# Gating the second FFN weight per batch instead of the FFN output, in an adaLN block on one Trainium2 core

## What is computed

```python
sa, ca, ga, sb, cb, gb = chunks of silu(c) @ wmod      # one row of 1024 for each batch
ga, gb = sign * max(|.|, 0.25)
h = layernorm(x) * (1 + ca) + sa
x = x + ga * gelu(h @ attn.T + b2_attn)                # attn = (w1 @ w2.T) * band mask
h = layernorm(x) * (1 + cb) + sb
P = h @ U1;  H = P @ V1 + b1                           # rank 256, 2 x 2752 columns
Z = (silu(gate) * up) @ U2                             # rank 256
x = x + gb * (Z @ V2 + b2f)                            # V2: 256 x 1024
```

## Time and profile before

| | us |
|---|---|
| median of 3 runs | 1271.64 |
| lowest, highest | 1271.54, 1274.2 |
| span of the profiled execution | 1272.8 |
| TensorE busy in it | 1200.2 |
| VectorE, ScalarE, GpSimd busy | 683.4, 388.0, 239.6 |

### The profile page before, as it was taken

How to read it: one execution, slowest core, us unless ns; L and a number is a source line. 1 busy time by engine, 2 the same in 40 slices (tenths; PEclk the granted TensorE clock), 3 DMA queues, 4 the chain that set the end, 5 groups by cost and what they waited for, 6 DMA issues and landing times.

```text
span 1272.8 us, 15879 instructions
## 1 busy us (share of the span) xinstructions
PE 1200.2 (94%) x5617; PEld 956.4 (75%) x5617; DVE 683.4 (54%) x1104; ACT 388.0 (30%) x645; POOL 239.6 (19%) x194
## 2 busy tenths in 40 slices
PE   7877999999999899999999989999999999999995
PEld 4445678877777688788878868878877887887884
DVE  0838699999996433453363353363353336336335
ACT  0122334444433454223322312223322331332230
POOL 0023322233222364120030030030011003003003
PEclk9899899999999899999999989999998999999998
DMA  9796644544447453050050031013004004003001
GB/s 347 280 382 242 238 166 182 214 181 181 192 181 272 169 169 124 28 176 1 1 182 1 1 119 64 1 57 126 1 24 160 1 1 162 20 1 115 35 1 66
DMA packets 51168, 154.71 MB, mean 122 GB/s; under 512 B 4640, under 2 KB 8992, under 8 KB 49056
## 3 DMA queue, kind: packets, MB, share of 16 engines
q1 hardware_dynamic: 51104, 153.79, 33.2%
HBM read 111.80 MB, written 41.98 MB: 121 GB/s over the span
## 4 chain that ended last, share of the span: by engine, by line
issue 56%; PE 24%; DVE 8%; POOL 8%; DMA 2%; ACT 1%; SPq 1%; POOLq 0%; DVEq 0%; ACTq 0%
POOL x2t L1360 6%; PE bank L469 5%; PE bank L471 5%; PE bank L470 5%; PE bank L539 4%; DVE nrm L1024 2%; PE bank L635 2%; DMA x<-in_x 2%; PE bank L504 1%; DVE bn L1182 1%; DVE h_lo L1125 1%; DVE bn L1014 1%; DMA wm_sb<-in_wmod 1%; POOL g L1308 1%; DVE xr L1177 1%
## 5 line engine op out<-in xcount | busy, mean ns | idle before, releaser
L1236 DVE SCALAR_TENSOR_TENSOR act<-bank,b_sb,act 128x512 f32<-128x512 f32 (+1 forms) x176 | 131.9, 750 | 411.9 <-PE bank L471 394.0
L961 ACT ACTIVATE act<-bank,b_sb 128x512 f32<-128x512 f32 (+1 forms) x176 | 121.3, 690 | 546.9 <-PE bank L471 529.3
L469 PE MATMUL bank<-pt,v_hi 128*128 128x512 f32 x688 | 270.9, 394 | 7.7 <-issue 6.2
L470 PE MATMUL bank<-pt,v_hi 128*128 128x512 f32 x688 | 269.7, 392 | 0.0
L471 PE MATMUL bank<-pt,v_lo 128*128 128x512 f32 x688 | 269.6, 392 | 0.0
L1360 POOL TENSOR_TENSOR x2t<-ffn,x2t 128x512 f32<-128x512 f32 x64 | 89.9, 1410 | 677.0 <-DVE ffn L1272 677.0
L469 PEld LDWEIGHTS bank<-pt,v_hi 128*128 128x128 f32 x688 | 130.2, 189 | 38.4 <-issue 9.6
L471 PEld LDWEIGHTS bank<-pt,v_lo 128*128 128x128 f32 x688 | 130.3, 189 | 27.3
L470 PEld LDWEIGHTS bank<-pt,v_hi 128*128 128x128 f32 x688 | 130.3, 189 | 26.8
L469 PE MATMUL bank<-act_hi,u_hi 128*128 128x512 f32 (+1 forms) x352 | 138.3, 393 | 0.9 <-DVE act_lo L1243 0.9
L471 PE MATMUL bank<-act_hi,u_lo 128*128 128x512 f32 (+1 forms) x352 | 137.0, 389 | 0.0
(11 more groups left out here) (111 smaller groups left out, 1519.5 us busy)
## 6 DMA issues: line engine op xcount, KB each, us to landing
wm_sb<-in_wmod SPq DMA_DIRECT2D x10, 2048.0 KB, 12.4
xr<-in_x SPq DMA_DIRECT2D x16, 1024.0 KB, 6.9
x_dram<-xr SPq DMA_DIRECT2D x16, 1024.0 KB, 4.4
x2t<-x_dram SPq DMA_DIRECT2D x32, 512.0 KB, 3.9
out<-x2t SPq DMA_DIRECT2D x32, 512.0 KB, 4.6
xs<-in_x SPq DMA_DIRECT2D x7, 2048.0 KB, 8.1
pt_dram<-pt_st SPq DMA_DIRECT2D x8, 1024.0 KB, 3.9
pt<-pt_dram SPq DMA_DIRECT2D x8, 1024.0 KB, 5.8
```

The costliest lines, as they stand in the source:

```text
L469: nc.tensor.matmul(acc, s_hi, m_hi, start=start, stop=False)
L470: nc.tensor.matmul(acc, s_hi, m_lo, start=False, stop=False)
L961: nc.scalar.activation(act[0:w, i % 2, :], bank[0:w, i % 2, :], ACT.Silu, bias=b1_sb[0:w, i, 0:1]).then_inc(silu_done, 1)
L1236: nc.vector.scalar_tensor_tensor(act[0:w, i % 2, :], up, b1_sb[0:w, i, 1:2], act[0:w, i % 2, :], ALU.add, ALU.mult).then_inc(act_done, 1)
```

## The change

- The gate row is multiplied into V2 for each batch. SP loads V2 into a buffer `v2g` for each batch; GpSimd multiplies it by the gate row in 4 parts of 128x512, ScalarE makes 4 high parts (`v2_hi_part`, after steps 16 to 19 of the batch), GpSimd 4 low parts. The two V2 pieces leave the weight queue. `out_product` waits for the 4 low parts of its batch.
- The row gb * b2f is computed once (`gbb2`), written to DRAM by eight small stores like the gate row, and read back broadcast for each batch. b2f comes to the core by eight small loads for this. GpSimd adds the row to the tile of x2 in place, 8 additions of 128x512 for a batch (`bias_x2`), after the low parts of V2.
- VectorE does one operation for a block: PSUM plus tile of x2, into the tile. The buffers `ffn` go, and so does the addition on GpSimd behind it.
- SP's order: loads for the next batch's V2 and rows are issued when this batch's low parts of V2 and its biased tile are done, ahead of this batch's output stores.

```diff
@@ names, sync engine @@
+            b2f_rows = c_pad[0:FB * NB].rearrange("p k c -> p (k c)")[:, 0:P]
+            gbb2_rows = b2f_rows
-        ffn = buf(p2, "ffn", [P, 3, HALF])
+        v2g = buf(p2, "v2g", [P, RB, D])
-        b2f_bc = buf(p2, "b2f_bc", [P, D])
+        gbb2_bc = buf(p2, "gbb2_bc", [P, D])
-        for h in range(NH):
-            pieces.append([(v2_view[:, :, h * HALF:(h + 1) * HALF], P, RB, HALF, 0,
-                            v2_hi[:, :, h * HALF:(h + 1) * HALF], v2_lo[:, :, h * HALF:(h + 1) * HALF])])
+        V2_PARTS = [(r, slice(h * HALF, (h + 1) * HALF)) for r in range(RB) for h in range(NH)]
+        V2_FROM = 16
             iteration(NB - 1, True, True, False, (), True)
+            sp.wait_ge(mod_mm, NCHUNK)
+            for k in range(FB):
+                sp.dma_start(b2f_rows[k * NB:(k + 1) * NB, :],
+                             b2f[:, k * P:(k + 1) * P].broadcast_to([NB, P])).then_inc(b2f_in, 16)
             for m in range(3, 7):
                 raw_load(m)
...
                 sp.dma_start(gb_dram[:, 0, k * P:(k + 1) * P], gb_rows[k * NB:(k + 1) * NB, :]).then_inc(gb_out, 16)
+            sp.wait_ge(gbb2_ready, 1)
+            for k in range(FB):
+                sp.dma_start(gbb2_dram[:, 0, k * P:(k + 1) * P],
+                             gbb2_rows[k * NB:(k + 1) * NB, :]).then_inc(gb_out, 16)
             for m in range(7, PIECES):
                 raw_load(m)
             sp.wait_ge(pt_out, 16 * NB)
-            sp.wait_ge(gb_out, 16 * FB)
-            sp.dma_start(b2f_bc[:], b2f[:, :].broadcast_to([P, D])).then_inc(b2f_in, 16)
+            sp.wait_ge(gb_out, 2 * 16 * FB)
+            def gates_in(b):
+                if not at_start(b):
+                    sp.wait_ge(v2_lo_ready, b * 4)
+                sp.dma_start(v2g[:], v2_view).then_inc(v2_in, 16)
+                sp.dma_start(gb_bc[:], gb_dram[b].broadcast_to([P, D])).then_inc(gb_in, 16)
+                if not at_start(b):
+                    sp.wait_ge(x2_biased, b * 8)
+                sp.dma_start(gbb2_bc[:], gbb2_dram[b].broadcast_to([P, D])).then_inc(gbb2_in, 16)
+            gates_in(0)
...
-                if not at_start(b):
-                    sp.wait_ge(ffn_ready, b * 8)
-                sp.dma_start(gb_bc[:], gb_dram[b].broadcast_to([P, D])).then_inc(gb_in, 16)
+                if not last:
+                    gates_in(b + 1)
@@ TensorE, out_product @@
-                pe.wait_ge(w_ready, PIECES)
+                pe.wait_ge(v2_lo_ready, b * 4 + 4)
-                        pe.wait_ge(ffn_sum, b * 8 + max(m - 1, 0))
+                        pe.wait_ge(out_ready, b * 8 + max(m - 1, 0))
@@ ScalarE @@
+            def v2_hi_part(b, part):
+                r, cols = V2_PARTS[part]
+                ae.wait_ge(v2_gated, b * 4 + part + 1)
+                if part == 0 and not at_start(b):
+                    ae.wait_ge(o_mm, b * 8)
+                nc.scalar.activation(v2_hi[:, r, cols], v2g[:, r, cols], ACT.Copy).then_inc(v2_hi_ready, 1)
                     act_hi_part(b, q, i - 1)
+                    if V2_FROM <= i < V2_FROM + 4:
+                        v2_hi_part(b, i - V2_FROM)
@@ VectorE @@
+            dve.wait_ge(gb_ready, 1)
+            dve.wait_ge(b2f_in, 16 * FB)
+            nc.vector.tensor_tensor(gbb2_rows, gb_rows[:], b2f_rows, ALU.mult).then_inc(gbb2_ready, 1)
...
-                        nc.vector.tensor_tensor(ffn[:, m % 3, :], bank[:, 6 + m % 2, :], b2f_bc[...], ALU.add)
-                        nc.vector.tensor_tensor(ffn[:, slot, :], ffn[:, slot, :], gb_bc[...], ALU.mult)
+                    half = x2t[:, n, h * HALF:(h + 1) * HALF]
+                    dve.wait_ge(o_mm, b * 8 + m + 1)
+                    dve.wait_ge(x2_biased, b * 8 + m + 1)
+                    nc.vector.tensor_tensor(half, bank[:, 6 + m % 2, :], half, ALU.add).then_inc(out_ready, 1)
@@ GpSimd @@
-                    nc.gpsimd.tensor_tensor(half, ffn[:, m % 3, :], half, ALU.add).then_inc(out_ready, 1)
+            def gate_v2(b):
+                pool.wait_ge(v2_in, b * 16 + 16)
+                pool.wait_ge(gb_in, b * 16 + 16)
+                for part, (r, cols) in enumerate(V2_PARTS):
+                    nc.gpsimd.tensor_tensor(v2g[:, r, cols], v2g[:, r, cols], gb_bc[:, cols],
+                                            ALU.mult).then_inc(v2_gated, 1)
+                for part, (r, cols) in enumerate(V2_PARTS):
+                    pool.wait_ge(v2_hi_ready, b * 4 + part + 1)
+                    nc.gpsimd.tensor_tensor(v2_lo[:, r, cols], v2g[:, r, cols], v2_hi[:, r, cols],
+                                            ALU.subtract).then_inc(v2_lo_ready, 1)
+            def bias_x2(b):
+                pool.wait_ge(gbb2_in, b * 16 + 16)
+                for m in range(TT * NH):
...
+                    nc.gpsimd.tensor_tensor(half, gbb2_bc[:, h * HALF:(h + 1) * HALF], half,
+                                            ALU.add).then_inc(x2_biased, 1)
+            with pool.Fori(0, NB) as b:
+                gate_v2(b)
+                bias_x2(b)
```

More of the change, by code:

```diff
@@ L75, in adaln_block @@
     gb_dram = nc.dram_tensor("gb_dram", [NB, 1, D], F32, kind="Internal").ap()
+    gbb2_dram = nc.dram_tensor("gbb2_dram", [NB, 1, D], F32, kind="Internal").ap()
     with ExitStack() as ctx:
@@ L251, in adaln_block @@
         o_mm = sem("o_mm")
-        ffn_sum = sem("ffn_sum")
-        ffn_ready = sem("ffn_ready")
+        v2_in = sem("v2_in")
+        v2_gated = sem("v2_gated")
+        v2_hi_ready = sem("v2_hi_ready")
+        v2_lo_ready = sem("v2_lo_ready")
+        x2_biased = sem("x2_biased")
         out_ready = sem("out_ready")
         b2f_in = sem("b2f_in")
+        gbb2_ready = sem("gbb2_ready")
+        gbb2_in = sem("gbb2_in")
         gb_in = sem("gb_in")
@@ L934, in weight_hi @@
                     ae.wait_ge(p_done, NB)
-                if m == PIECES - NH:
-                    ae.wait_ge(pt_out, 16 * NB)
                 ae.wait_ge(raw_in[m % 3], raw_count[m])
@@ L1256, in batch @@
                     multiply(b + 1, 1 - q, 0)
[L1257 to L1273, removed]
+                for m in range(TT * NH):
+                    n, h = m // NH, m % NH
+                    half = x2t[:, n, h * HALF:(h + 1) * HALF]
+                    dve.wait_ge(o_mm, b * 8 + m + 1)
+                    dve.wait_ge(x2_biased, b * 8 + m + 1)
+                    nc.vector.tensor_tensor(half, bank[:, 6 + m % 2, :], half, ALU.add).then_inc(out_ready, 1)
                     if m == 3 and not last:
@@ L1351, in _ @@
                 weight_lo(m)
-            def residual(b):
+            def gate_v2(b):
[10 more added lines that the diff above has]
+                pool.wait_ge(gbb2_in, b * 16 + 16)
                 for m in range(TT * NH):
@@ L1358, in residual @@
                         pool.wait_ge(x2t_in[n], b * 16 + 16)
-                    pool.wait_ge(ffn_ready, b * 8 + m + 1)
-                    nc.gpsimd.tensor_tensor(half, ffn[:, m % 3, :], half, ALU.add).then_inc(out_ready, 1)
+                    nc.gpsimd.tensor_tensor(half, gbb2_bc[:, h * HALF:(h + 1) * HALF], half,
+                                            ALU.add).then_inc(x2_biased, 1)
             with pool.Fori(0, NB) as b:
-                residual(b)
+                gate_v2(b)
+                bias_x2(b)
 _NAMES = ["x", "w1", "w2t", "b2", "mask", "u1", "v1", "u2", "v2", "b1_main", "b1_tail", "b2f", "ct", "wmod"]
```

## The result

| | before | after |
|---|---|---|
| median of 4 runs, us | 1272.92 | 1254.85 |
| lowest, highest | 1271.54, 1274.69 | 1254.12, 1255.44 |
| span of the profiled execution | 1272.8 | 1252.3 |
| TensorE, VectorE, ScalarE, GpSimd busy | 1200.2, 683.4, 388.0, 239.6 | 1193.5, 672.5, 402.4, 320.1 |

The ratio is 0.986, with a 95% interval of 0.9847 to 0.9874. The change makes the kernel 18.1 us faster.

The account below looks back on a forecast made before the run. TensorE, busy for 94% of the span, was taken to bound the kernel. The terms -9.3 - 6.8 + 5.6 + 1.2 = -9.3 us took the median of 1271.64 to 1262.3 us; range 1256 to 1268.5.

Parts of the forecast that it names:

- output stage, batches 0 to 6: Output products: with one VectorE addition for each block, the 1.33 us lost per batch all goes, -9.3 us (bounds -9.3 and -6.4).
- low parts beside GpSimd: Batch's last two activations: GpSimd's new work stretches VectorE's low parts, TensorE 0.7 us late in 8 batches, +5.6 us (0 to 8.8).
- tail: After the last batch's products: last addition ends at 1262.9, the GpSimd addition behind it gone, -6.8 us (-5 to -8).
- start of the second phase: Near 458 us: eight more small stores delay weight piece 7, so TensorE waits, +1.2 us (0 to 2; 4.9 with slow clock).
- loop's returns: Loop iteration ends: 3.15 us gap and 2.95 us slow clock at the one read, both left unchanged, 0 us.
- The change touches neither, so I leave both: Step on TensorE's loop return: 3.15 us gap without releaser and 2.95 us slow clock taken as unaffected by the change.
- Rival (d): Output stage: loss stays because GpSimd's multiplications stretch VectorE's inserted operations; 1265.2 us; chance 0.70 together with the forecast.
- Rival (c): Steps 20 and 21: GpSimd's eight additions block VectorE until the last ends, 28 us instead of 5.6, 1284.7 us; chance 0.09.
- Rival (a): Last low parts of a batch: GpSimd does not delay them, so without the 5.6 us, 1256.7 us; chance 0.11.
- Rival (b): Whole kernel: upper ends of both costs (8.8, 4.9) with lower gains (6.4, 5) eat the gain, about 1271 us; chance 0.10.

## Why the prediction was wrong

Against the profiled spans, 1272.8 and 1252.3, term by term:

| term | predicted, us | measured, us | from |
|---|---|---|---|
| output stage, batches 0 to 6 | -9.3 | -9.3 | 7 x (101.06 - 99.73) |
| low parts beside GpSimd | +5.6 | +3.4 | 8 x (100.15 - 99.73) |
| tail | -6.8 | -8.5 | 23.42 - 14.92 |
| start of the second phase | +1.2 | 0 | no wait near 458 us |
| loop's returns | 0 | -5.5 | 12.13 - 6.60 |
| sum | -9.3 | -19.9 | spans: -20.5 |

The 0.6 us left arise before the second phase: behind its first wait TensorE starts at 443.15 us in the kernel before and at 442.51 in the changed one. The medians differ by 18.1 rather than 20.5 us, as the spans are of one execution each, and the changed kernel's profiled execution is the fastest of its four (1254.12). The tail's slow clock, 1.7 us, is in one of the two executions and not in the other.

- **The step that failed** is "The change touches neither, so I leave both", on gap and slow clock at the loop's return. I had taken a gap without a releaser for a constant. It depends on what SP's stores and tile loads are doing, and the change moves these: a block no longer passes through two VectorE operations and a GpSimd addition before its tile is stored, but through one VectorE operation, so that the store and the load behind it start earlier. The first tile's store is issued 7.4 us ahead of the first gap instead of 4.9. Holding stores back alone shortened the gaps, one block later lengthened them, and writing the loop out removed them. 5.5 of the 10.6 us that the sum was short lie here. That is not one lucky execution: by their periods the two returns cost 6.6 us in the changed kernel, 5.2 with earlier bias additions and 6.6 with more small stores. The traces also show the fetch: one 16 KB transfer of the instruction queue at each return, 1.67 us ahead of TensorE's next matmul (table at the end). With 6.6 us for the two returns instead of 12.1 the forecast's own terms come to -14.8 us. That is 1256.8 us on the median I forecast from, inside the range.
- **Output stage**: right, to 0.01 us a batch. Products take 10.88 us, the block's addition 0.69, and the inserted operations delay nothing. The experiment without the bias confirms the reading that VectorE's second operation, stretched as it is, was the cause. Rival (d), a stall that stays, is out.
- **Low parts**: the mechanism was right, the size off. GpSimd and VectorE alternate as in the earlier trace rows, and the pair takes 2.88 us. I had put 0.7 us a batch between 0 and 1.1; it is 0.42. The phase of the eight additions was laid out wrongly, as they take 11.8 and not 10.3 us and start at 616.76, not 618.4 (1.1 us of this is that everything lies earlier: block 0 starts at 632.05 and not at 633.19). Two steps of the working do not follow from their rows either: from 618.4 in steps of 1.29 us an addition ends at 624.85 and one at 626.14, none at 625.8; and the four normalisations of the earlier trace rows take 5.88 / 4 = 1.47 us each, not 1.52. Rival (c), the train, did not come: VectorE got in after each operation. Rival (a) did not either, but moving the additions 16 us earlier makes it true. The Trainium skill's GPSIMD Engine Reference, Key points, says that VectorE instructions with two SBUF inputs contend with GpSimd. This trace agrees: 2.88 us for the pair instead of 1.46. By the Trainium skill's Advanced Engine Details and Errata, Mode Summary, alone the pair would still take 1.46 us, and it does not.
- **Tail**: the store chain went as laid out, 6.8 us; the rest, 1.7 us, is the slow clock of blocks 0 and 1 that the earlier trace rows show before and that is absent after, with the same idle time of 2.01 us in front. The two written-out kernels, neither of which has it, confirm the first part: 21.82 and 14.99 us from the first output product to the end. Of the ten profiled executions six have this slow clock and four do not, with kernels of both kinds on either side and 2.01 us of idle time in all, so the 1.7 us are luck of the two executions and no effect of the change that I can show.
- **Start**: the chain was right and the price of its first link wrong. I took the eight new stores at the present eight's 4.63 us; they took 2.67. By source line the present eight hold one of 1.55 us (1.72 in the changed kernel) beside others of 0.33 at the median, and the new eight took 0.29 to 0.30 each: I had taken one long issue for a property of all. With eight more, the predicted wait appeared at 459 us, slow clock included.
- **Rival (b)**, the gain eaten, had its parts at the wrong end: low parts, tail and start all came out on the gain's side.
- The chances put 0.81 on faster, and that held. The range did not: it had no room for the returns, although the prediction itself reads 3.15 + 2.95 = 6.1 us at one of them, 12.1 us at the two, which is more than any wait of TensorE in the second phase that the profile puts down to an engine (6.9 us for VectorE in all).

The Trainium skill, Runtime: NRT & Kernel Launch, Instruction fetch mechanics, says that a taken branch whose target is not at hand forces a DMA fetch before execution goes on, and that this is a reason to write loops out. The runs here agree: a 16 KB transfer of the instruction queue ends 1.67 us before TensorE goes on, the returns cost 12.1 us by the periods, and the kernel before, written out, takes 1259.9 instead of 1273.7 us on the same chip. Had I weighed it, I would have asked which transfers are under way at 746 us.

## What to carry to other kernels

An idle gap with no releaser in the profile is not a constant. If it lies at a loop's return, look for the transfer of the instruction queue and at which other transfers are under way as the gap begins, before and after the change; if TensorE's instruction stream allows it, write the loop out. When an elementwise operation moves to GpSimd, place its train where the VectorE operations with two SBUF inputs have slack, not at the end of a batch. Before the price of a group is carried over to new instructions, look at its members: one long one can make up a third of the sum.

## What the hardware showed unexpectedly

- Each of the 14 gaps at TensorE's loop return (seven kernels, two returns) has one 16 KB transfer of queue q8, kind instruction, and TensorE goes on 1.66 to 1.68 us after its end. The transfer takes 0.88 to 0.89 us in 12 of them (1.05 and 1.39 in the others), so the gap's length is set by when it starts:

| kernel | gaps, us | start of the transfer from the gap's start, us | tile transfers as the gap begins |
|---|---|---|---|
| before, stores held | 2.33, 1.92 | -0.72, -0.62 | none |
| changed | 2.27, 2.10 | -0.27, -0.62 | ending |
| changed, earlier bias additions | 2.27, 2.38 | -0.29, -0.17 | ending |
| changed, more small stores | 2.19, 2.27 | -0.36, -0.28 | ending |
| before | 3.15, 3.07 | +0.58, +0.51 | about 2 us more |
| changed, stores one block later | 3.63, 3.66 | +1.08, +1.12 | 1.2 us more |
| before, without the bias | 3.79, 3.75 | +1.24, +1.21 | 1.6 us more |

That the fetch stands in line behind the packets of the tiles fits these rows but is not shown. How much they delay it does not grow with how long they go on: the kernel before has the longest overlap and the shortest of the long gaps.

- Behind each gap of 3.07 us and more, or already in it, TensorE's clock fell to 0.50; of the eight gaps of 1.92 to 2.38 us two were followed by a fall. Behind the idle time of 2.01 us ahead of the last output stage it fell in six of ten executions. A fall cost 1.6 to 3 us.
- One of eight small stores of one form took 1.55 us to issue, nearly five times the median of 0.33; in the changed kernel it is 1.72. What it waited for the trace does not show.
